# Reflector scaling, triangular squarings and input statistics issued beside the eigenvalue search and the twisted factorisation

## What is computed

```python
deg = sum(A, 0) + sum(A, 1) - diagonal(A)
L_norm = d_inv_sqrt[:, None] * (diag(deg) - A) * d_inv_sqrt[None, :]
_, U = eigh(L_norm)                       # 128 x 128
agg = einsum('mn,bnd->bmd', U.T, relu(layernorm(x)))
out = einsum('nm,bmd->bnd', U, relu(agg @ W1 + b1) @ W2 + b2)
```

## Time and profile before

| | us |
|---|---|
| median of 3 runs | 1551.87 (1549.56 to 1552.9) |
| the profiled execution | 1552.13 |
| its span | 1550.2 |

### The profile page before, as it was taken

How to read it: one execution, slowest core, us unless ns; L and a number is a source line. 1 busy time by engine, 2 the same in 40 slices (tenths; PEclk the granted TensorE clock), 3 DMA queues, 4 the chain that set the end, 5 groups by cost and what they waited for, 6 DMA issues and landing times.

```text
span 1550.2 us, 21586 instructions
## 1 busy us (share of the span) xinstructions
PE 1120.2 (72%) x5134; PEld 701.8 (45%) x5134; DVE 1040.5 (67%) x4180; ACT 693.6 (45%) x1760; POOL 306.1 (20%) x1038
## 2 busy tenths in 40 slices
...
DMA packets 16655, 12.30 MB, mean 8 GB/s; under 512 B 665, under 2 KB 14530, under 8 KB 16578
## 3 DMA queue, kind: packets, MB, share of 16 engines
...
...
## 4 chain that ended last, share of the span: by engine, by line
PE 51%; DVE 33%; issue 7%; ACT 5%; DVEq 1%; DMA 1%; ACTq 0%; POOL 0%; POOLq 0%
PE P L1363 30%; PE P L709 10%; PE P L1512 3%; DVE scal L337 2%; ACT arena L677 2%; DVE arena L460 2%; DVE bst_all L929 2%; DVE arena L510 2%; DVE arena L512 1%; ACT hb L1174 1%; DVE arena L464 1%; DVE bcol L366 1%; DVE arena L458 1%; PE P L1505 1%; DVE arena L343 1%
## 5 line engine op out<-in xcount | busy, mean ns | idle before, releaser
L1363 PE MATMUL P<-arena,WT 128*128 (+2 forms) x792 | 329.1, 580 | 3.9 <-ACT L1262 2.9
L1363 PEld LDWEIGHTS P<-arena,WT 128*128 128x128 f32 x792 | 152.0, 192 | 180.9 <-issue 167.1
L709 PE MATMUL P<-arena 1*128 1x127 f32 (+62 forms) x504 | 163.1, 431 | 80.6 <-ACT arena L677 56.6
L1275 ACT ACTIVATE arena<-P,bl 128x512 f32<-128x512 f32 (+1 forms) x252 | 153.6, 636 | 139.1 <-PE P L1363 131.7
L709 PEld LDWEIGHTS P<-arena 1*128 1x128 f32 x504 | 124.2, 307 | 132.7 <-DVE arena L347 109.2
L918 POOL COPY arena<-arena 128x512 f32<-128x512 f32 x16 | 21.2, 1367 | 680.3 <-DVE arena L1095 588.5
L1084 DVE TENSOR_TENSOR arena<-arena 128x512 f32<-128x512 f32 (+1 forms) x36 | 22.0, 611 | 137.5 <-ACT arena L1275 137.5
L669 ACT ACTIVATE arena<-arena 1x127 f32<-1x127 f32 (+62 forms) x126 | 32.2, 256 | 155.0 <-DVE arena L358 144.7
L1174 ACT ACTIVATE hb<-xN,nmr,rsd 128x128 f32 (+1 forms) x192 | 78.5, 481 | 34.9 <-PE P L1363 28.1
L197 POOL TENSOR_SCALAR lf<-lf 1x1 f32<-1x1 f32 x210 | 85.6, 408 | 21.9
L709 PE MATMUL P<-arena,Ib 128*128 128x46 bf16 (+1 forms) x318 | 34.4, 269 | 63.4 <-ACT arena L696 62.9
...
## 6 DMA issues: line engine op xcount, KB each, us to landing
...
```

Of the source, the lines that this page charges most:

```text
L709: def mm(o,l,r,start=True,stop=True): return t.matmul(o,lhsT=l,rhs=r,start=start,stop=stop)
L1275: act(s.gt[u][gate][:,0:cols],P[4*u+gate][:,0:cols],f,bias=s.bl[:,4*(p-1)+gate:4*(p-1)+gate+1]).then_inc(ev('lstm_gates'),1)
L1363: def mm(o,l,r,start=True,stop=True,**k): return t.matmul(o,lhsT=l,rhs=r,start=start,stop=stop,**k)
```

## The change

- The two instructions that square and clamp the reflector norms go into steps 4 and 6 of the first search pass on VectorE, the reciprocal and the scaling into steps 4 and 6 of the second (`reflector_scale`). Their square root goes ahead of half 0 in ScalarE's program, with a wait for the input x.
- Behind the search TensorE transposes and multiplies the reflectors; VectorE does only the mask multiply, at step 12 of the factorisation. All other copies of the squarings are ScalarE's. M and N share one tile `MN`, copied at once; additions and subtractions are done on TensorE with the identity as a second matmul into the same bank. On ScalarE the root of sweep 14 stands behind the first copy, the root of sweep 15 behind QT.
- The statistics are no longer bn_stats. ScalarE sums each tile by a Copy with accumulator, two after every half of the search (`input_mean`), and behind the root of sweep 15 it sums the squared deviations of the 64 tiles (`input_deviations`, Square with bias and accumulator). Their full-size outputs go to tiles that are unused then. VectorE makes the variance in one instruction.
- X's transpose comes from a second product of Yt and QT in place of a transpose of X. The variance stands ahead of X's copy on VectorE, the bias columns behind it, the Newton step of the scale behind the copy of XT.
- ScalarE no longer waits for U and the biases ahead of its first tiles, and its table load there is gone.

```diff
@@ -439,6 +439,13 @@
...
         two=lambda t: t.rearrange("p (t w) -> p t w",t=2)
+        def reflector_scale(pass_,i):
+            if (pass_,i)==(0,4): c.mark(ttr(tmp[:,:],refl[:,:],refl[:,:],deg[:,20:21]))
+            elif (pass_,i)==(0,6): ts(deg[:,20:21],deg[:,20:21],0.5,1e-30,ALU.mult,ALU.max).then_inc(ev('norm2'),1)
+            elif (pass_,i)==(1,4):
+                v.wait_ge(ev('norm'),1)
+                c.mark(v.reciprocal(deg[:,22:23],deg[:,21:22]))
+            elif (pass_,i)==(1,6): ts(refl[:,:],refl[:,:],deg[:,22:23],None,ALU.mult).then_inc(ev('reflectors_unit'),1)
         def count_below(pass_,first):
@@ -460,6 +467,7 @@
...
                 if i%2: leaf_at(HH_SPOTS+HN//2*pass_+i//2)
+                else: reflector_scale(pass_,i)
                 c.wait(b)
@@ -501,6 +509,9 @@
...
             j=N-1-i
+            if i==REFLECTOR_MASK:
+                v.wait_ge(ev('reflector_products'),1)
+                stt(M[0],P[3][:,0:N],-1.0,below[:,:],ALU.mult,ALU.mult).then_inc(ev('M_ready'),1)
             if i%2 and HH_SPOTS+HN+i//2<=SPOTS*(SWEEPS-1)+10: leaf_at(HH_SPOTS+HN+i//2)
@@ -580,50 +591,19 @@
...
-        c(ttr(tmp[:,:],refl[:,:],refl[:,:],deg[:,20:21]))
-        c(ts(deg[:,20:21],deg[:,20:21],0.5,1e-30,ALU.mult,ALU.max))
-        v.sem_inc(ev('norm2'),1)
-        v.wait_ge(ev('norm'),2)
-        c(v.reciprocal(deg[:,22:23],deg[:,21:22]))
-        ts(refl[:,:],refl[:,:],deg[:,22:23],None,ALU.mult).then_inc(ev('reflectors_unit'),1)
-        v.wait_ge(ev('reflectors_T_psum'),1)
-        v.tensor_copy(refl_T[:,:],P[0][:,0:N]).then_inc(ev('reflectors_T'),1)
-        v.wait_ge(ev('reflector_products'),1)
-
-        c(tt(M1[:,:],P[1][:,0:N],below[:,:],ALU.mult))
-        v.sem_inc(ev('M_N_copied'),1)
-        v.wait_ge(ev('reflector_products'),2)
-        c(v.tensor_copy(N1[:,:],P[2][:,0:N]))
-        v.sem_inc(ev('M_N_copied'),1)
-        v.wait_ge(ev('reflector_products'),3)
-        c(tt(Z[:,:],refl[:,:],P[3][:,0:N],ALU.subtract))
-        M=[M1,M2]
-        Nn=[N1,N2]
-        v.wait_ge(ev('x_in'),64)
-        for s in range(6):
-            a,b=s%2,(s+1)%2
-            net.input_stats(v,11*s,6)
-            v.wait_ge(ev('squares'),s+1)
-            c(v.tensor_copy(M[b][:,:],P[1][:,0:N]))
-            c(v.tensor_copy(Nn[b][:,:],P[2][:,0:N]))
-            v.sem_inc(ev('squares_copied'),1)
-            net.input_stats(v,11*s+6,5)
-            v.wait_ge(ev('power_times_Z'),s+1)
-            c(tt(Z[:,:],Z[:,:],P[3][:,0:N],ALU.add))
-            v.sem_inc(ev('Z_grown'),1)
-        v.wait_ge(ev('Q_correction'),1)
-        c(tt(QT[:,:],I[:,:],P[1][:,0:N],ALU.subtract))
-        c(v.tensor_copy(Yt[:,:],P[0][:,0:N]))
-        v.sem_inc(ev('QT_ready'),1)
+        v.wait_ge(ev('Y_T_psum'),1)
+        v.tensor_copy(Yt[:,:],P[0][:,0:N]).then_inc(ev('Y_T'),1)
+        net.input_variance(v)
         v.wait_ge(ev('X_psum'),1)
-        c(v.tensor_copy(X[:,:],P[2][:,0:N]))
-        v.sem_inc(ev('X_ready'),1)
+        v.tensor_copy(X[:,:],P[2][:,0:N]).then_inc(ev('X_ready'),1)
+        net.bias_columns(v,c)
         for q in range(2):
...
             v.wait_ge(ev('A_times_X'),q+1)
-            c(v.tensor_copy(A_X[:,:],P[3][:,0:N]))
-            if q==0: c(v.tensor_copy(XT[:,:],P[0][:,0:N]))
-            v.sem_inc(ev('W_ready'),1)
+            v.tensor_copy(A_X[:,:],P[3][:,0:N]).then_inc(ev('W_ready'),1)
+            if q==0:
+                c.mark(v.tensor_copy(XT[:,:],P[0][:,0:N]))
+                net.input_scale(v,c)
             v.wait_ge(ev('S_and_G'),q+1)
@@ -685,6 +664,9 @@
...
             a.activation(same[h%2][:,:],P[h%2][:,0:SEG//2*2*W],ACT.Abs).then_inc(ev('sturm_same'),1)
+        a.wait_ge(ev('norm2'),1)
+        a.activation(deg[:,21:22],deg[:,20:21],ACT.Sqrt).then_inc(ev('norm'),1)
+        a.wait_ge(ev('x_in'),64)
         for h in range(2*HALVES):
...
             q0=((SEG+2)*g+(SEG//2+1)*u)*2*W
@@ -696,13 +678,26 @@
...
             if h%HALVES==HALVES-1: shared_signs(h)
-        for sweep in range(SWEEPS):
-            if SPOTS*sweep+8-HH_SPOTS>=HN: leaf_root_of(sweep)
-        a.wait_ge(ev('norm2'),1)
+            net.input_mean(a,2*h,2)
+        a.wait_ge(ev('reflectors_T_psum'),1)
+        a.activation(refl_T[:,:],P[2][:,0:N],ACT.Copy).then_inc(ev('reflectors_T'),1)
+        late=[sweep for sweep in range(SWEEPS) if SPOTS*sweep+8-HH_SPOTS>=HN]
+        leaf_root_of(late[0])
+        a.wait_ge(ev('reflector_products'),2)
+        a.activation(Nn[0],P[2][:,0:N],ACT.Copy).then_inc(ev('reflectors_T'),1)
+        a.wait_ge(ev('power_times_Z'),1)
+        a.activation(Z[:,:],P[3][:,N:2*N],ACT.Copy).then_inc(ev('Z_grown'),1)
+        for q in range(6):
+            a.wait_ge(ev('squares'),q+1)
+            a.activation(MN[(q+1)%2][:,:],P[2][:,0:2*N],ACT.Copy).then_inc(ev('squares_copied'),1)
+            a.wait_ge(ev('power_times_Z'),q+2)
+            a.activation(Z[:,:],P[3][:,N:2*N],ACT.Copy,scale=-1.0 if q==5 else 1.0).then_inc(ev('Z_grown'),1)
+        a.wait_ge(ev('reflector_products'),3)
+        a.activation(QT[:,:],P[2][:,2*N:3*N],ACT.Copy).then_inc(ev('QT_ready'),1)
+        for sweep in late[1:]: leaf_root_of(sweep)
+        net.input_deviations(a)
+        a.wait_ge(ev('norm2'),2)
         a.activation(pair_state[:,1:2],pair_state[:,4:5],ACT.Sqrt).then_inc(ev('norm'),1)
-        a.wait_ge(ev('norm2'),2)
-        a.activation(deg[:,21:22],deg[:,20:21],ACT.Sqrt).then_inc(ev('norm'),1)
-        a.wait_ge(ev('U_ready'),2)
         net.scalar(a)
@@ -764,48 +759,46 @@
...
+        t.wait_ge(ev('reflectors_unit'),1)
+        t.transpose(P[2][:,0:N],refl[:,:],I[:,:]).then_inc(ev('reflectors_T_psum'),1)
+        t.wait_ge(ev('reflectors_T'),1)
+        mm(P[3][:,0:N],refl_T[:,:],refl_T[:,:]).then_inc(ev('reflector_products'),1)
+        t.wait_ge(ev('M_ready'),1)
+        t.transpose(P[2][:,0:N],M[0],I[:,:]).then_inc(ev('reflector_products'),1)
+        mm(P[3][:,N:2*N],I[:,:],refl[:,:],stop=False)
+        mm(P[3][:,N:2*N],M[0],refl[:,:],start=False).then_inc(ev('power_times_Z'),1)
+        t.wait_ge(ev('reflectors_T'),2)
+        for q in range(6):
+            a,b=q%2,(q+1)%2
+            mm(P[2][:,0:N],Nn[a],M[a])
+            mm(P[2][:,N:2*N],M[a],Nn[a]).then_inc(ev('squares'),1)
+            t.wait_ge(ev('squares_copied'),q+1)
+            t.wait_ge(ev('Z_grown'),q+1)
+            mm(P[3][:,N:2*N],I[:,:],Z[:,:],stop=False)
+            mm(P[3][:,N:2*N],M[b],Z[:,:],start=False).then_inc(ev('power_times_Z'),1)
+        t.wait_ge(ev('Z_grown'),7)
+        mm(P[2][:,2*N:3*N],I[:,:],I[:,:],stop=False)
+        mm(P[2][:,2*N:3*N],Z[:,:],refl[:,:],start=False).then_inc(ev('reflector_products'),1)
         t.wait_ge(ev('leaf_sign'),1)
...
+        t.wait_ge(ev('eigenvalue_diagonal'),1)
+        mm(P[5][:,0:N],ones[:,:],wide[:,0:N]).then_inc(ev('eigenvalue_row'),1)
         t.wait_ge(ev('Y_ready'),1)
...
+        t.transpose(P[0][:,0:N],Y[:,:],I[:,:]).then_inc(ev('Y_T_psum'),1)
         t.wait_ge(ev('QT_ready'),1)
+        t.wait_ge(ev('Y_T'),1)
         mm(P[2][:,0:N],QT[:,:],Yt[:,:]).then_inc(ev('X_psum'),1)
+        mm(P[0][:,0:N],Yt[:,:],QT[:,:])
         for q in range(2):
...
+            if q==0: t.wait_ge(ev('X_ready'),1)
             else: t.wait_ge(ev('U_ready'),1)
...
+            t.wait_ge(ev('eigenvalue_diagonal'),q+2)
+            mm(P[3][:,0:N],ones[:,:],wide[:,0:N]).then_inc(ev('eigenvalue_row'),1)
             t.wait_ge(ev('correction'),q+1)
@@ -966,13 +955,41 @@
...
+  def input_mean(s,a,first,count):
+
+    for b in range(first,first+count):
+        a.activation(s.unused_slot(a,b),s.xN[:,b*N:(b+1)*N],ACT.Copy,scale=-1.0/N,accum_out=s.nt[:,b:b+1]).then_inc(s.ev('input_sums'),1)
+  def unused_slot(s,a,n):
+    if n>=16: a.wait_ge(s.ev('input_sums'),n-15)
+    return (s.ob+s.yb)[n//4%4][:,n%4*N:(n%4+1)*N]
+  def input_deviations(s,a):
+    a.wait_ge(s.ev('input_sums'),NB)
+    for b in range(NB):
+        a.activation(s.unused_slot(a,NB+b),s.xN[:,b*N:(b+1)*N],ACT.Square,bias=s.nt[:,b:b+1],accum_out=s.nt[:,3*NB+b:3*NB+b+1]).then_inc(s.ev('input_sums'),1)
+  def input_variance(s,v):
+    v.wait_ge(s.ev('input_sums'),2*NB)
+    v.tensor_scalar(s.nt[:,NB:2*NB],s.nt[:,3*NB:4*NB],1.0/N,1e-5,ALU.mult,ALU.add).then_inc(s.ev('layer_variance'),1)
+  def input_scale(s,v,c):
+    nt=s.nt
+    a,b_,cc,d=(nt[:,i*NB:(i+1)*NB] for i in range(4))
+    v.wait_ge(s.ev('layer_root'),1)
+    s.newton_root(v,c,b_,cc,d)
+    v.tensor_tensor(s.nmr[:,:],a,s.rsd[:,:],ALU.mult).then_inc(s.ev('layer_scale'),1)
+  def newton_root(s,v,c,b_,cc,d):
+    c(v.reciprocal(d,cc))
+    c(v.tensor_tensor(d,d,b_,ALU.mult))
+    c(v.tensor_tensor(d,d,cc,ALU.add))
+    c(v.tensor_scalar(d,d,0.5,None,ALU.mult))
+    c(v.reciprocal(s.rsd[:,:],d))
+  def bias_columns(s,v,c):
     ev=s.ev
...
+    v.wait_ge(ev('row_sums'),1)
+    c(v.tensor_copy(s.BC[:,:],s.P[6][:,N:N+s.NR+16]))
+    c.mark(v.tensor_tensor(s.bl[:,:],s.bcol('bih',16),s.bcol('bhh',16),ALU.add))
+    v.wait_ge(ev('b2_in'),32)
```

(60 more changed lines are left out.)

30 lines of the change are left out of this document (6 added, 24 removed).

## The result

| kernel | median us | launches | ratio to before |
|---|---|---|---|
| before | 1552.38 | 1549.56 to 1552.99 (4) | |
| changed | 1537.28 | 1532.15 to 1538.65 (4) | 0.9891 [0.9852, 0.993] |

The number in round brackets is that of the launches, the bracket behind a ratio its 95% interval. The change gains 15.1 us where 29 were forecast, and 1537.28 lies above the range. The profiled execution took 1537.32 us, span 1535.57 against 1550.24.

The account below looks back on a forecast made before the run. VectorE was taken to bound search and factorisation, with one dependent thread from 631.6 to 690.2 us. 1552.1 less 32.1 saved plus 3.3 paid gave 1523.3, or 1523.2 us as median (64%); range 1519.5 to 1528.5.

Parts of the forecast that it names:

- Step 1: Middle stretch, Y to X: only Y's transpose and copy remain, so the X product starts 25.66 us earlier.
- Step 2: X to first trace sum: now holds bias and scale work on VectorE; sum 24.83 us earlier, 24.9 saved so far.
- Step 3: Last update of U to first mix: ScalarE's tiles lie ready, saving 7.2 us; 32.1 saved in all.
- Step 4: Search and factorisation: longer VectorE wait at sweep 11's root 2.7, second-pass scaling 0.3, mask multiply 0.25; 3.3 us paid.
- Steps 5 and 6: Beside the factorisation, squarings (slack 3.4 us) and 64 ScalarE deviations fit, as do the search's means: cost 0.
- the squarings' rival: Slower ScalarE-TensorE hand-offs make the squarings hold sweep 15's leaf root; VectorE waits 3.2 us, 1526.4 us; 10%.
- the accumulator's: Rival: accumulator read adds in full, 0.67 us each; sweep 11's root 2.5 us later, 1525.7 us; 10%.
- the overrun: Rival: 64 accumulating squares delay Y's square root; at 1.2 us an instruction, 1555 us; 3%.
- small instructions that slow down: Rival: VectorE's some 500 one-column factorisation instructions slow beside busy engines, 5 ns each, 2.5 us, 1525.8 us; 7%.
- The sum up to the first mix: Everything ahead of the first mix: 32.1 us saved in the middle stretch less 3.3 paid in search and factorisation.
- the last line of the sum: Whole kernel: 1552.1 - 32.1 + 3.3 = 1523.3 us, with nothing counted for the loops behind the first mix.
- The rival of an early clock: At the first mix: TensorE, busier ahead of it, has its clock up early, 1521.5 us; 6%.

Follow-up runs that it names:

- scale_late: The changed kernel with bias columns and the first scale's Newton step put back behind the last update of U; 1542.05 us (one launch).
- root_first: The changed kernel with the reflector root and first input sums put behind the leaf root of sweep 11; 1535.86 us, ratio 0.9885 to before.
- root_first_p11: The changed kernel with sweep 11's leaf root ahead of the input sums, plus two 128x512 ScalarE copies ahead of attention; 1526.65 us, ratio 0.9821 to before.
- root_first_dense1: The changed kernel with sweep 11's leaf root ahead of the input sums, plus one unused product per attention-times-value group; 1528.06 us, ratio 0.9839 to before.
- after_p11: The changed kernel with two 128x512 ScalarE copies added ahead of the first attention tiles; 1524.54 us, ratio 0.9835 to before.
- before_p11: The kernel before with two 128x512 ScalarE copies added ahead of the first attention tiles; 1560.83 us, ratio 1.0041 to before.
- before_p04: The kernel before with one 128x360 ScalarE copy added ahead of the first attention tiles; 1568.14 us, ratio 1.0102 to before.

## Why the prediction was wrong

- **Step 1 (Y to X), right.** Forecast 1.20 us from Y's write to the X product, measured 1.29.
- **Step 2 (X to the trace sum), right.** Forecast 5.0 with VectorE behind, measured 4.44 without a gap. Its bias and scale instructions do hold the sum: in scale_late it comes 4.88 us after Y's write in place of 5.73.
- **Step 3 (U to the mix), right.** Forecast 7.2 saved, measured 7.55 - 0.61 = 6.9. scale_late shows where it comes from: there the mix starts 5.24 us behind UT's write.
- **Step 4 (the search pays), mis-sized.** The cause was right: root_first takes it away, and the root stands 4.23 us behind the last weight copy again. But the delay of the root was forecast at 2.7 us net and is 1.59. An accumulating activation costs 0.29 to 0.30 us to the next one and not 0.36, the reflector root 0.09 and not 0.20, so 2.45 us went in and not 3.1; and 0.86 of them were absorbed, not 0.4: ScalarE's 0.56 us of waiting for TensorE went in full, and 0.3 more. The scaling and the mask multiply cost 0.38 us (from the reciprocal to Y's write) for 0.55. With the weight copy 0.25 us earlier, Y came 1.71 us later in the profile, where 3.3 were forecast.
- **Steps 5 and 6, right.** A round took 2.54 us for 2.6. From 555.6 on it took 1.63, since the clock rose, and QT was 3 us early. A deviation took 0.38 us for 0.45, and the last ended at 594.7. Neither the squarings' rival nor the accumulator's nor the overrun came, and the 0.38 us of step 4 leave no room for small instructions that slow down by 2.5 us. (The 3.4 us of slack, called 16% of the chain, are 18% of its 19.2 us.)
- **The sum up to the first mix:** 28.8 forecast, 30.6 measured.
- **The step that failed** is the last line of the sum. It set everything behind the first mix equal to before, and the prediction said that it is wrong "if the loops behind the first mix take another time than before". They did, by 15.9 us. Of these, 1.6 lie between the mix and the attention. The rival of an early clock had the sign wrong: TensorE was busy 9.70 us of the 28.02 ahead of the mix (35%; before 24.19 of 58.6, 41%), and the clock rose 5.1 us behind the mix and not 2.9. The share alone doesn't give this: root_first, root_first_p11 and root_first_dense1 come to the mix by the same program, and the clock rises 5.4, 3.4 and 3.3 us behind it. As the same stage also took 676.5 and 677.5 us in two profiles of the changed kernel, how much of the 1.6 is the edit's stays open. And 14.3 are three falls of the clock in an attention whose code is the same. No rival had this, though the earlier trace rows show that TensorE's clock isn't constant. I treated the rounds of a loop without an edit as fixed in length, and they are only at a fixed clock.

Without falls the sum holds: after_p11 gave 1522.1 to 1524.6 in three of four launches. The kernel before paid nothing like this in 27 of the 32 launches that stood beside all these kernels (1549.17 to 1552.99). The other five were 1559.1, 1559.4 and 1566.6 to 1569.1. These are the lengths of before_p11 and before_p04. Their granted clock over the launch, 0.871 to 0.878, is nearly that of the long launches of those two (0.872 to 0.878 in seven of ten); in the 23 shorter launches of before for which it is on record it is 0.880 to 0.884 in 19. So two or three falls are likely there too, but no profile was taken of them. By their lengths the changed kernel pays in all ten of its launches: one at 1532.15, nine from 1535.9 to 1538.7.

Still open: what sets the place of the attention against the clock, and by what the place decides; why the changed kernel comes to the distance of 671.3 to 671.4 nearly every time and before to 672.0, and what differs between two launches of root_first_p11. Also whether one product a group prevents falls at the distance of 671.35; it wasn't tried there.
